# Early-fusion block: the first attention's softmax divided behind its weighing, with a new order of steps on every engine

## What is computed

```
xr  = layernorm(h) @ W_reduce + b_reduce
q, k, v = split(xr @ W_qkv + b_qkv)          # 12 heads of 8, segments of 24 tokens
p   = exp((q @ k.T - max) * scale);  p = p / sum(p)
h   = h + concat(p @ v) @ W_proj + b_proj
```

## Time and profile before

| | us |
|---|---|
| median of 3 runs | 353.9 (352.41 to 355.89) |
| the profiled execution | 353.93 |
| its span in the profile | 352.1 |
| TensorE busy in the span | 329.2 (93%) |
| VectorE busy | 204.2 (58%) |
| ScalarE busy | 100.9 (29%) |
| GpSimd busy | 50.5 (14%) |
| mean granted clock of TensorE | 0.993 |

### The profile page before, as it was taken

The page is one execution under the profiler, slowest core; times in us unless marked ns, Lnnn a source line. Parts: engine busy times, 40 slices in busy tenths (PEclk is TensorE's granted clock), DMA queues, the critical chain, the costliest instruction groups (busy, mean ns, idle before and its releaser), DMA issues. The chain is left out here.

```text
span 352.1 us, 7993 instructions
## 1 busy us (share of the span) xinstructions
PE 329.2 (93%) x3292; PEld 234.9 (67%) x3292; DVE 204.2 (58%) x639; ACT 100.9 (29%) x210; POOL 50.5 (14%) x119
## 2 busy tenths in 40 slices
PE   3899999998799899999999999999999999997975
PEld 3676567786574458678595867758867675775564
DVE  5936388999988952243325324332525476888545
ACT  1233557876433510101011010101021234322440
POOL 8604252332111020000000000000111020110100
PEclk9999999999999999999999999999999999999989
DMA  7993010522600029993487130000000000000005
GB/s 257 345 234 104 4 58 17 136 77 63 159 16 1 2 54 197 186 238 85 143 193 169 38 98 0 3 0 3 0 2 0 2 2 0 3 2 0 2 1 134
DMA packets 27804, 26.65 MB, mean 76 GB/s; under 512 B 4118, under 2 KB 22936, under 8 KB 27768
## 3 DMA queue, kind: packets, MB, share of 16 engines
q1 hardware_dynamic: 26871, 25.55, 29.0%
q10 hardware_dynamic: 896, 0.59, 0.7%
HBM read 24.86 MB, written 1.28 MB: 74 GB/s over the span
## 5 line engine op out<-in xcount | busy, mean ns | idle before, releaser
L736 PEld LDWEIGHTS banks<-sb_wo_sl,sb_attn_hidT_attn 128*128 128x128 f32 x384 | 62.2, 190 | 5.6 <-issue 4.9
L736 PE MATMUL banks<-sb_wo_sl,sb_attn_hidT_attn 128*128 128x192 f32 x384 | 64.5, 328 | 0.0
L1714 DVE COPY sb_w_tok_e_out<-banks 60x384 f32<-60x384 f32 x32 | 17.8, 555 | 49.8 <-PE banks L736 49.3
L1242 ACT ACTIVATE sb_attn_hidT_attn<-banks 128x480 f32<-128x480 f32 x24 | 13.6, 571 | 102.9 <-PE banks L723 102.9
L718 PE MATMUL banks<-sb_tok_xeT,sb_wi_sl 128*128 128x480 f32 x96 | 40.1, 567 | 1.1 <-ACT sb_tok_xeT L1227 1.1
L1704 DVE TENSOR_SCALAR sb_attn_hidT_attn<-banks 128x480 f32<-128x480 f32 x24 | 15.8, 658 | 27.9 <-PE banks L723 25.9
L718 PEld LDWEIGHTS banks<-sb_tok_xeT,sb_wi_sl 128*128 128x128 f32 x96 | 18.0, 190 | 18.9 <-issue 17.0
L503 PE MATMUL banks<-sb_tok_xeT 128*32 128x193 f32 (+1 forms) x512 | 24.8, 328 | 0.0
L723 PE MATMUL banks<-sb_tok_xeT,sb_wi_sl 64*128 64x480 f32 x96 | 21.5, 580 | 0.0
L503 PEld LDWEIGHTS banks<-sb_tok_xeT 128*32 128x32 f32 (+1 forms) x512 | 16.8, 109 | 6.5 <-issue 3.6
L474 POOL MEMSET sb_attn_hidT_attn<- 1x384 f32 x1 | 0.4, 413 | 119.6 <-PE banks L736 119.6
(11 more groups left out here) (239 smaller groups left out, 540.1 us busy)
## 6 DMA issues: line engine op xcount, KB each, us to landing
sb_wo_sl<-in_wo SPq DMA_DIRECT2D x16, 288.0 KB, 4.1
sb_tok_xeT<-in_xin SPq DMA_DIRECT2D x8, 448.0 KB, 6.0
sb_onehot_combT<-route_rows SPq DMA_DIRECT2D x6, 512.0 KB, 8.8
sb_wi_sl<-in_wi SPq DMA_DIRECT2D x8, 288.0 KB, 3.4
sb_wi_sl<-in_wi SPq DMA_DIRECT2D x24, 96.0 KB, 3.4
sb_xn<-route_rows SPq DMA_DIRECT2D x4, 512.0 KB, 11.3
sb_w_tok_e_out<-in_wtok SPq DMA_DIRECT2D x2, 960.0 KB, 7.3
sb_attn_hidT_attn<-route_rows SPq DMA_DIRECT2D x2, 512.0 KB, 12.2
```

The lines of the kernel that those rows point to most:

```text
L736: mm = nc.tensor.matmul(PS[:, 4 + j // 2, j % 2 * D:(j % 2 + 1) * D], hidT[:, e % 2, f, j * 128:(j + 1) * 128], wo_sl[:, q, f], start=(f = ...
L1242: nc.scalar.activation(hidT[:, e % 2, f].rearrange("f (g c) -> f g c", g=PAIRS)[:, :, 0:CAP], PS[:, HID_BANKS[f], 0:SLOTS].rearrange("f (g ...
L1714: ve.tensor_copy(e_out[64 * (e % 2):64 * (e % 2) + CAP, hf * 4 + z:hf * 4 + z + 3:2, e // 2], PS[64 * z:64 * z + CAP, 4 + hf, 0:2 * D].rea ...
```

## The change

1. `score_norm` (three VectorE instructions for each j and g, twelve times) is gone. `turn_weights` waits for the exponential, and turns and weighs weights that are not yet divided.
2. `weigh_values(j)` is one step for all three head groups. It first issues three matmuls (32 by 384) of a constant block matrix `head_ones` with the turned weights, which leave in bank 2, for each of 96 channels and each token, the sum of that head's weights. Then come the 48 weighing matmuls with g as the innermost loop, so that consecutive ones go to different 32 rows of PSUM.
3. On VectorE, `sum_scales(j)` takes the reciprocal of the 96 by 384 sums, and `keep_outputs(j)`, formerly a copy on ScalarE, multiplies the weighed values with it on their way out of PSUM.
4. GpSimd sets up `head_ones` with five more small memsets. `ssum` is gone, `o_scale` [96, 384] and `head_ones` [128, 32] are new.
5. The lists of steps of TensorE, ScalarE and VectorE are laid anew, from the patch stage to the end.

```diff
             def turn_weights(j, g):
-                pe.wait_ge(sem("a_prob"), NGRP * j + g + 1)
+                pe.wait_ge(sem("a_exp"), NGRP * j + g + 1)
...
-            def weigh_values(j, g):
-                if g == 0:
-                    pe.wait_ge(sem("a_vexp"), 9 * j + 9)
-                    pe.wait_ge(sem("a_vexp_late"), 2 * SEGS * (j + 1))
-                pe.wait_ge(sem("a_probT"), NGRP * j + g + 1)
+            def weigh_values(j):
+                pe.wait_ge(sem("a_vexp"), 9 * j + 9)
+                pe.wait_ge(sem("a_vexp_late"), 2 * SEGS * (j + 1))
+                pe.wait_ge(sem("a_probT"), NGRP * j + NGRP)
+                for g in range(NGRP):
+                    mm = nc.tensor.matmul(PS[g * 32:g * 32 + 32, 2, 0:TOK], head_ones[:],
+                                          probT[:, g].rearrange("k b (s t) -> k b s t", s=SEGS)[:, :, :, 0:SEG],
+                                          start=True, stop=True)
+                mm.then_inc(sem("a_total_ps"), 1)
                 for b in range(4):
                     for s in range(SEGS):
                         at = b * N + s * SEG
-                        mm = nc.tensor.matmul(PS[g * 32:g * 32 + 32, 3, at:at + SEG], v_exp[:, j % 2, b, s, g * 32:g * 32 + 32],
-                                              probT[:, g, b, s * 32:s * 32 + SEG], start=True, stop=True)
-                if g == NGRP - 1:
-                    mm.then_inc(sem("a_oT_ps"), 1)
+                        for g in range(NGRP):
+                            rows = slice(g * 32, g * 32 + 32)
+                            mm = nc.tensor.matmul(PS[rows, 3, at:at + SEG], v_exp[:, j % 2, b, s, rows],
+                                                  probT[:, g, b, s * 32:s * 32 + SEG], start=True, stop=True)
+                mm.then_inc(sem("a_oT_ps"), 1)
...
-            def score_norm(j, g):
-                n = NGRP * j + g
-                ve.wait_ge(sem("a_exp"), n + 1)
-                ve.tensor_reduce(ssum[:, g], prob_view(j, g), AX_X, ALU.add).then_inc(sem("a_sum"), 1)
-                ve.wait_ge(sem("a_sum"), 2 * n + 1)
-                ve.reciprocal(ssum[:, g], ssum[:, g]).then_inc(sem("a_sum"), 1)
-                ve.wait_ge(sem("a_sum"), 2 * n + 2)
-                ve.tensor_tensor(prob_view(j, g), prob_view(j, g), ssum[:, g].unsqueeze(2).to_broadcast(every_key), ALU.mult
-                                 ).then_inc(sem("a_prob"), 1)
+            def sum_scales(j):
+
+                ve.wait_ge(sem("a_total_ps"), j + 1)
+                ve.reciprocal(o_scale[:], PS[0:C1, 2, 0:TOK]).then_inc(sem("a_sum"), 1)
+
+            def keep_outputs(j):
+                ve.wait_ge(sem("a_sum"), j + 1)
+                need(ve, "a_proj_ps", j - 2)
+                ve.wait_ge(sem("a_oT_ps"), j + 1)
+                ve.tensor_tensor(oT[0:C1, j % 3].rearrange("c (x b t) -> c x b t", x=NB, b=4),
+                                 PS[0:C1, 3, 0:TOK].rearrange("c (b x t) -> c x b t", b=4, x=NB),
+                                 o_scale[:].rearrange("c (b x t) -> c x b t", b=4, x=NB), ALU.mult).then_inc(sem("a_oT"), 1)
```

In layer 1 the lists change by single steps. In TensorE's, for one:

```diff
             keep_busy(0, 512, 2)
+            turn_soft(2)
+            keep_busy(0, 256)
             linear_outputs(3)
-            turn_soft(2)
+            soft_logits(2)
             linear_project(3, 0)
-            soft_logits(2)
             linear_project(3, 1)
             soft_inputs(2)
-            keep_busy(0, 256)
             soft_hidden(0, 3)
```

More of the change, by code:

```diff
@@ L408, in _ @@
                 then(gp.memset(qmask[QB * b:QB * b + QB, b:b + 1], 1.0))
+            then(gp.memset(head_ones[:], 0.0))
+            for r in range(GRP):
+                then(gp.memset(head_ones[32 * r:32 * r + 32, HDIM0 * r:HDIM0 * r + HDIM0], 1.0))
             for a in (0, 64):
@@ L933, in _ @@
             reduce_inputs(0)
+            square_sums(1)
             patches(2, 1)
@@ L942, in _ @@
             square_rows(3)
+            free(a_qT=1)
+            turn_inputs(1)
             free(tok_mid=4, tok_var=4)
             scores(0)
-            turn_inputs(1)
             free(tok_mid=6, tok_var=6)
             patches(3, 0)
+            free(x_ss=4)
+            turn_weights(0, 0)
+            square_sums(3)
+            free(a_xnT=2)
+            reduce_inputs(1)
             free(a_sub=3)
             turn_projection()
-            free(a_xnT=2)
-            reduce_inputs(1)
             patches(3, 1)
@@ L954, in _ @@
             keys(1)
-            square_sums(3)
-            turn_weights(0, 0)
-            route_projection()
+            free(a_vexp=9)
+            turn_weights(0, 1)
             queries(1)
@@ L960, in _ @@
             values(1)
+            route_projection()
             free(a_kexp=8, a_qT=2)
             turn_inputs(2)
-            free(a_vexp=9)
-            turn_weights(0, 1)
             free(col_router=1)
@@ L970, in _ @@
             reduce_inputs(2)
[L971 to L974, removed]
+            weigh_values(0)
             free(a_xl=3)
@@ L983, in _ @@
             turn_weights(1, 0)
+            free(a_kexp=12, a_qT=3)
+            turn_inputs(3)
             turn_weights(1, 1)
@@ L986, in _ @@
             scores(2)
[L987 to L989 removed]
+            free(a_probT=4)
+            turn_weights(1, 2)
             free(a_vexp=27)
             count_choices(0)
[L992 to L995 removed]
+            weigh_values(1)
+            free(a_oT=2)
+            project(1)
             free(a_xnT=4)
             reduce_inputs(3)
[L998 to L999 removed]
             free(a_h=2, r_part=2)
             turn_weights(2, 0)
+            turn_weights(2, 1)
+            free(a_xl=4, a_xrT=4)
+            keys(3)
+            queries(3)
+            free(a_probT=7)
+            turn_weights(2, 2)
             free(r_counted=1)
             values(3)
[L1004 to L1010 removed]
             free(a_sub=9)
             scores(3)
[L1013 removed]
             free(a_vexp=36)
             count_choices(1)
[L1016 removed]
+            weigh_values(2)
             free(a_oT=3)
@@ L1019, in _ @@
             dispatch(0)
+            free(a_h=3, r_part=3)
+            turn_weights(3, 0)
+            turn_weights(3, 1)
             free(r_counted=2)
@@ L1893, in _ @@
             keep_projection()
-            score_norm(0, 2)
             token_write(6)
@@ L1899, in _ @@
             score_max(1, 1)
+            sum_scales(0)
+            keep_outputs(0)
+            first_norm(3)
             score_max(1, 2)
-            score_norm(1, 0)
-            first_norm(3)
-            score_norm(1, 1)
             add_attention(0)
@@ L1947, in _ @@
             choose(3)
+            route_norm(2)
             route_norm(3)
+            place(3)
             scale_routes(3)
-            place(3)
             mark_slots(2)
@@ L2007, in _ @@
             key_norms(3)
+            add_linear(2, 0)
             soft_max(1)
-            add_linear(2, 0)
+            token_shift(1)
+            add_linear(2, 1)
+            soft_moments(2)
             slot_weights(1)
-            add_linear(2, 1)
-            token_shift(1)
-            soft_moments(2)
             query_norms(3)
+            soft_norm(2)
             norm_products(3)
```

208 lines of the change are left out of this document (88 added, 120 removed).

## The result

| | before | after |
|---|---|---|
| median, four runs each on one chip | 354.84 us (352.41 to 355.89) | 361.45 us (361.27 to 362.11) |
| span of the profiled execution | 352.1 us | 359.8 us |
| first expert matmul | 122.76 us | 130.80 us |

The ratio is 1.0205, 95% interval 1.0162 to 1.0247 (the quotient of the two medians is 1.0186): the change makes the kernel slower by about 2%. The whole of it is there at the first expert matmul, which comes 8.0 us later; behind it the profiled execution is 0.3 us shorter than the one before.

A forecast was written before the change was run, and what follows sets the result against it. It took VectorE to bound the attention stage and TensorE the experts. 353.9 + 3.0 (attention stage to first expert) - 0.7 (layer 1) + 1.8 (TensorE's clock) = 358.0 us, range 352.5 to 362.5, the forecast's own 356 to 361.

The forecast's parts named there:

- to `add_attention(0)`: VectorE up to the first add_attention: later scores, two norms gone, reciprocal and multiplication added; +1.1 us.
- lap 1: VectorE from add_attention(0) to add_attention(1): 11.9 us before, 11.65 forecast, entered as -0.3 us.
- lap 2: VectorE from add_attention(1) to add_attention(2): 14.05 us before, 15.3 forecast with waits for projection and counts, +1.2 us.
- lap 3: VectorE from add_attention(2) to add_attention(3): 12.2 us before, 12.8 forecast, +0.6 us.
- to `dispatch(2)`: From the last add_attention to TensorE's dispatch(2): VectorE's slack gone and one more keep_busy, +0.4 us.
- TensorE's clock: Clock falls behind three new waits ahead of project(1) to project(3), about 1.3 us each; bounds 0 and 3.9, taken +1.8 us.
- layer 1: New order behind the experts, slot_weights(2) ahead of both add_linear(3): -0.7 us, between -2 and +1.
- The reciprocal: VectorE's reciprocal of 96 by 384 sums, four times: 2.5 us each by slope, bounds 0.55 and 3.2 us.
- TensorE's savings: Sums 0.8 us and weighing 1.3 against 3.3 before: 1.2 us less for each j, but not on the path.
- The rival with the clock holding: The chain costs as summed but TensorE's clock holds everywhere: 356.2 us, chance 0.21.
- the worse end: Rival: reciprocal takes 3.2 us and the clock falls in all three waits: 363.1 us, chance 0.10.
- The planner's view: Rival: VectorE's whole saving of 4.1 us counts, waits are filled and TensorE follows: 350.3 us, chance 0.12.

The follow-up runs named there:

- all-warm kernel: Changed kernel with matmuls on constants in TensorE's waits ahead of project(1), project(2), project(3) and in two short waits of lap 2: 356.27 us, ratio 1.0027.
- one-step weighing alone: Kernel before with only the three groups' weighing in one interleaved step: 357.17 us; with constant matmuls added ahead of scores(3): 352.79 us.
- group-by-group run: Changed kernel with exp(-ln(sum)) on ScalarE, its weighing matmuls ordered group by group, still in one step: 355.88 us, ratio 1.0028.
- `reduce_inputs(3)` earlier: Changed kernel with reduce_inputs(3) moved ahead of project(1), and two ScalarE steps moved ahead of exp_scores(2, 2): 361.05 us, ratio 1.0159.
- ScalarE's version: Changed kernel with the reciprocal replaced by exp(-ln(sum)) on ScalarE: 348.83 us; with reduce_inputs(3) ahead of project(1) as well: 348.32 us.
- layer 1's order alone: Kernel before with only the new orders of TensorE, ScalarE and VectorE behind the experts: 353.71 us, ratio 0.998.

## Why the prediction was right in its direction and short in its size

Forecast 358.0 us, +4.1 on 353.9; measured 361.45, half a microsecond above the forecast's own range of 356 to 361. Of the 3.4 us between the two, 0.9 is the base: the prediction took the median of three runs, and the median of four is 354.84. The change itself is +6.6 us between the medians and +7.7 between the profiled executions. The terms, against the latter, with the all-warm kernel to part chain from clock:

| term | forecast | shown |
|---|---|---|
| to `add_attention(0)` | +1.1 | +1.4 |
| lap 1 | -0.3 | -0.25 |
| lap 2 | +1.2 | +1.4 |
| lap 3 | +0.6 | +0.5 |
| to `dispatch(2)` | +0.4 | +0.5 |
| from there to the first expert | 0 | +0.1 |
| TensorE's clock | +1.8 | +4.3 |
| layer 1 | -0.7 | -0.3 |

Both profiled executions have a fall of the clock ahead of the end, at `soft_inputs(3)` before and during it after, so the last row is not layer 1's order at full clock.

**The reciprocal** was the right suspect and nearly the right size: 2.55 us against 2.5. The slope of the narrow ones carries to 384 columns, (2550 - 253) / 368 = 6.2 ns an element. The Trainium skill, VectorE: DVE Perf Modes, section "First, the fixed hardware budget", would give 3.2 us by my estimate of eight VectorE cycles an element; the trace is 20% below that, and the measurement decides. The copy in its place shows what a plain pass would have made of the change.

**The chain.** The steps named in the prediction are the ones in the trace: reciprocal and multiplication stand ahead of `add_attention` with nothing between for j = 2 and 3, and at full clock the four `add_attention` stand at 69.5, 81.2, 96.7 and 109.4 us where the text had 69, 81, 96 and 109.

**TensorE's savings** came as costed (sums 0.85 us, weighing 1.2). That they were worth nothing on the changed kernel's path, also as said, is read from its trace: the reciprocal starts beside the weighing and ends behind it (93.73 + 2.54 us against 92.58 + 1.18). What the text did not see is that they can be worth less than nothing: the one-step weighing alone cost 0.75% by the clock. That the interleaving matters is shown by the group-by-group run, 2.99 against 1.2 us.

**The step that failed is the clock term**: "Bounds 0 and 3.9 us; I take 1.8, a little under half, since the phase of each wait is open." The waits were named rightly (2.5 to 3 us; they are 2.84, 3.25 and 2.81), and so was the pair that prices a fall. But the fall was entered at a little under half its price, with only the open phase for a reason, and the clock fell in all three. Behind each the half clock lasted over the projection and the step behind it: 0.9, 1.8 and 1.1 us on laps 1 to 3 and 0.6 up to `dispatch(2)`, 4.3 in all, the upper bound and a little more. My own sentence had said that all three waits were longer than the one behind which the clock had fallen before; with that row the upper bound was the better choice. The rival with the clock holding was given 0.21 and is refuted. Of the worse end, the falls came true and the reciprocal of 3.2 us didn't.

**Slips in the working.** The terms of lap 3 add up to 12.73 us, not 12.8, so that lap was forecast at +0.5, as it came. No row gives the 8 ns an element of the upper bound; the steepest slope in the rows is 6. And 64 patch matmuls of 0.33 us in 2.96 us are seven at a time, not four; the 1.3 us for the weighing did not hang on it. None of the three moves the sum by more than 0.1 us.

**The planner's view**, in which VectorE's savings count, is refuted for this change. Once the reciprocal is not on VectorE its number is reached and passed (348.8 us against 350.3), but not its mechanism in full: VectorE then has 13.5 us less to do than before (190.7 against 204.2), and the time is 5.5 us shorter.

**What stays open**: why the clock falls behind one wait of 2.20 us and not behind another, and in some executions of a kernel and not in others; whether layer 1's new order gains anything; and why lap 2, which at full clock is 1.4 us longer than before, is so. The one attempt at it, `reduce_inputs(3)` earlier, was covered by the clock in the changed kernel, and where ScalarE divides it shortened the lap by 0.3 us.

## What to carry to other kernels

Dividing behind a contraction saves passes over the larger array, but a wide reciprocal on VectorE costs over four plain passes, and it moves from a place beside the matmuls onto the chain between two of them: look at who waits for it, and whether an idle ScalarE can do it as exp(-ln(x)). Where TensorE is the nearly full engine, price each new wait twice, once for itself and once for the half clock behind it, and where the trace has a fall behind a shorter wait, take the fall as the likelier case: here it came behind all three new ones. And count work on TensorE that fills a wait as free: taking it away can make a kernel slower, and constants put in its place delayed no step of the laps in the runs here. Last, when two kernels are within 1%, look at the granted clock of each execution before comparing medians.

## What the runs showed of the hardware that was not expected

- The length of a single wait does not tell whether the clock falls. Behind 1.53 us (`project(0)`), and behind 2.10 us ahead of the first weighing in both kernels with the one-step weighing alone, it held; behind 1.20 us, with another of 1.37 us shortly ahead, it fell (`reduce_inputs(3)` earlier). In lap 2 of ScalarE's version it fell behind three waits of 0.28, 0.60 and 0.89 us within six microseconds, between short matmuls. Behind the 2.20 us (2.21 in the kernel before) at the end it fell in nine kernels' traces and not in four, and at different points: `soft_inputs(3)`, 1.55 us at full clock, took between 1.67 (changed kernel) and 2.88 us (all warm), as less or more of it ran at half clock.
- It also differs between executions of one kernel. The 71 of the kernel before that ran beside the experiments fall into three groups: 9 with a granted clock of 1.000 at 352.45 to 353.02 us, 25 with 0.994 or 0.995 at 353.95 to 354.82, and 37 with 0.989 or 0.990 at 355.08 to 357.03. The steps are about 1.5 us, near the price of one fall (1.3 us by the earlier trace rows). The profiled one is of the middle group, and its one fall is at the end; where the second fall of the third group lies no trace shows.
- The twelve executions of layer 1's order alone lie the same way: three at 351.9 to 352.1 us with 0.998 or 0.999, and seven of the eight at 353.5 to 354.3 with 0.994 or 0.995. The eighth, at 353.47, had 1.000, so the clock is not all of it.
- Matmuls of 24 columns over all 128 rows, sent in turn to three blocks of 32 output rows, took 12.5 ns a record against 31 in one block at a time. The Trainium skill, TensorE: Matmul & The Clock Gate, section "The mechanism", says that a weight load overlaps a running matmul only where their row groups differ; here all share the rows and differ in the columns, and the two and a half times that interleaving gains does not come from differing row groups.
- ln and exp on ScalarE, 96 by 384, took 0.49 and 0.52 us back to back, with nothing else between them in the trace.
